# One wait of VectorE a step further back, and four split tiles of eight for three, in the edge stage of a graph network layer

## Chip, cores, metric

The kernel runs on one core of one Trainium2 chip. The metric is the device time of one execution in microseconds (us), here the median of several runs. The engines are TensorE (PE in the profile), VectorE (DVE), ScalarE (ACT), GpSimd (POOL) and SyncE (SP, which issues DMAs). The "PEld" rows of the profile are the weight loads of TensorE.

## What is computed

One layer of a graph network on 1250 nodes with 512 features and 20000 edges with 128 attributes, sorted by their target node:

```python
h = maximum(layernorm(x), 0)                    # node features
msg = relu(h[src] + (edge_attr @ W_edge + b_edge))
aggr = segment_sum(msg, dst, num_segments=N)    # the edge part
g = (1.0 + eps) * h + aggr
g = gelu(layer_norm(g @ W1 + b1, g1, be1))
g = gelu(layer_norm(g @ W2 + b2, g2, be2))
g = layer_norm(h + g, gA, bA)
m = gelu(g @ M1) @ M2
out = x + layer_norm(g + m, gB, bB)
```

Everything is float32. The first three lines are the edge part, with which this text deals; the dense stages follow it.

## The kernel before

**Tiles and groups.** An edge tile is 128 edges. There are 157 of them, in 40 groups of four (the last group has one tile). A group has two pairs of tiles; pair number 2 x group + p, with p 0 or 1, is what one instruction of 128x1024 elements handles. All loops over the groups are written out, so what an engine does stands in a fixed order.

**What happens to a pair.**
- GpSimd gathers the 128 source rows of each tile with an indirect DMA (L630) into `rows`, which has room for three groups. It waits for the z of six pairs back.
- TensorE embeds the pair: `embed` multiplies the attributes by W_edge into one of three PSUM buffers (`ps_u0`, `ps_u1`, `ps_t1`), and waits for the z of three pairs back, which read that buffer.
- VectorE adds the rows to the embedding: `add_rows` writes z (L1161). z has four buffers of a pair each.
- ScalarE makes `msg_hi`, relu(z) rounded to fp32r (L837). VectorE makes `msg_lo`, relu(z) minus msg_hi (L1167).
- TensorE scatters: `visit` (L1422) multiplies `msg_lo` and `msg_hi` by a one-hot matrix that ScalarE builds from the targets (apart L760, onehot L766), and sums into a window of 128 nodes in PSUM. Where a group straddles two windows there is a second one-hot matrix (apart_first L773) and more scatter matmuls, and ScalarE closes one window and opens the next (L784, L797). There are nine such groups: 12, 17, 21, 25, 28, 30, 33, 35 and 37.

**Two ways to embed a tile.** One matmul in fp32 (L1404), which leaves two records of 128x512 in the profile, one for each pass; or three in fp32r (L1386 to L1388), on attributes and weights that were split into a high and a low part. Of the four pairs of two groups (an even one and the odd one behind it), the first tile of the first `SPLIT` pairs goes the second way; all others the first. The split of these tiles is made for two groups at once: ScalarE rounds the attributes to `attr_hi` (L707), VectorE subtracts it from them into `attr_lo` (L1053). Groups 0 and 1 are not split.

**Order on the engines.** VectorE does, in a group: z of pair 0, msg_lo of the pair two before it, in even groups the split of the group two ahead, z of pair 1, msg_lo of the pair two before that. A z waits for the gathered rows, for the embedding, and, since z has four buffers, for a msg_lo (`msg_lo_done`). TensorE does, in a step: the scatter of pair 1 of two groups back, the embedding of pair 1 of the next group and of pair 0 of the one behind it, and the scatter of pair 0 of the group before.

Of the kernel before, what the change touches and what calls it, by code (L numbers as in the profile page):

```python
# [12 lines left out]
ZRING = 4  # L13
ATTRS = 6
ATTR_PAIRS = ATTRS // 2
SPLIT = 3
NG = 4 * -(-EDGES // (4 * EG))
ET = NG * TPG
TP = ET // 2
# [74 lines left out]
def build(nc, A, out):  # L94
# [10 lines left out]
    with ctx:  # L105
        def sb(name, shape, dt=f32, scope=ctx):
            return scope.enter_context(nc.sbuf_tensor(name, shape, dt))

        def sem(name):
            return ctx.enter_context(nc.semaphore(name))  # L110
# [72 lines left out]
        attr_raw = sb("attr_raw", [P, ATTRS, EG], f32, edge)  # L183
        attr_hi = sb("attr_hi", [P, 2, SPLIT * P], f32r, edge)
        attr_lo = sb("attr_lo", [P, 2, SPLIT * P], f32r, edge)
        apart = sb("apart", [P, TPG, P], f32, edge)
# [90 lines left out]
        z_done, msg_hi_done, msg_lo_done = (sem(n) for n in ("z_done", "msg_hi_done", "msg_lo_done"))  # L277
# [82 lines left out]
        def embedded(g, p):  # L360

            return (ps_u[0], ps_u[1], ps_t[1])[g.bank(p)][:, 0:D * g.in_pair(p)]

        def summed(g, p):

            return z[:, (2 * g.k + p) % ZRING, 0:D * g.in_pair(p)]

        def apart_tiles(k):
            return attr_raw[:, k:k + 2, :].rearrange("p g (u e) -> p (g u) e", e=2 * P)[:, 0:SPLIT, 0:P]

# [614 lines left out]
        def _(dve):  # L985
# [167 lines left out]
            def add_rows(g, p):  # L1153
                if g.gr == 0:
                    dve.wait_ge(direct_done, 2 * p + 2)
                else:
                    dve.wait_ge(rows_in[g.slot(p)], 32 * g.lap + 16 * g.in_pair(p))
                dve.wait_ge(emb_done[p], g.gr + 1)
                if 2 * g.gr + p >= 3:
                    dve.wait_ge(msg_lo_done, 2 * g.gr + p - 2)  # L1160
                v.tensor_tensor(summed(g, p), embedded(g, p),  # L1161
                                rows[:, g.r, 2 * p:2 * p + g.in_pair(p), :].rearrange("p a d -> p (a d)"), ALU.add).then_inc(z_done, 1)

# [6 lines left out]
            def group(g):  # L1170
                add_rows(g, 0)
                if not zero(g.gr):
                    msg_low(g.next(-1), 0)
                if g.gr % 2 == 0 and g.gr + 2 < NG:
                    split_attr(g.next(2))
                if g.pairs == 2:
                    add_rows(g, 1)
                if not zero(g.gr):
                    msg_low(g.next(-1), 1)
# [201 lines left out]
        def _(pe):  # L1381
# [8 lines left out]
            def embed(g, p):  # L1390
# [9 lines left out]
                for e in range(g.in_pair(p) - 1, -1, -1):  # L1400
                    place, second = g.half
                    part = 2 * second + p
                    if e or direct or part >= SPLIT:
                        last = t.matmul(o[:, e * D:(e + 1) * D], attr_raw[:, g.k, (2 * p + e) * P:(2 * p + e + 1) * P], we_raw[:, :],  # L1404
# [278 lines left out]
```

## Time and profile before

| | us |
|---|---|
| median of 3 runs | 490.02 (489.7 to 490.27) |
| the profiled execution | 489.55 |
| its span, first to last instruction | 487.5 |
| PE busy | 460.0 |
| DVE busy | 393.1 |
| ACT busy | 310.5 |
| POOL busy | 267.0 |

The edge part lasts up to about 241 us of the span. A row of the profile's timeline gives an instruction's start and how long it took. On VectorE and ScalarE an instruction can start before the one ahead of it has ended, so the distance from start to start tells more than the length. On TensorE a matmul's end is modelled, and again the starts are what counts. "Idle before" is what the profile shows an engine to have waited, with what released it.

### The profile page before, as it was taken

To read this page: it belongs to the slowest core of one execution; us is meant where nothing else is said; L and a number is where in the kernel's file an instruction comes from. 1 tells how busy PE (TensorE), PEld (TensorE's weight loads), DVE (VectorE), ACT (ScalarE), POOL (GpSimd) and SP (SyncE) were. 2 spreads that over 40 slices of the span, in tenths; PEclk is the share of its full clock that TensorE was granted. 3 is DMA by queue.
4 is the path that set the end of the run, shared out by engine and by line. 5 is a ranking of instruction groups with operands and counts; after the bars stand their busy time and mean duration, and the time that the engine had idled before them with its cause. 6 is when DMAs were issued, how large, how long until landed. Compare 5 with 4: busy or idle time off the path is not lost.

```text
span 487.5 us, 7358 instructions
## 1 busy us (share of the span) xinstructions
PE 460.0 (94%) x1927; PEld 340.2 (70%) x1928; DVE 393.1 (81%) x563; ACT 310.5 (64%) x586; POOL 267.0 (55%) x299
## 2 busy tenths in 40 slices
PE   6629999999999999999899999999999999999994
PEld 2205666666666666666678888888888898888883
DVE  6898899999999999899847777789989755752575
ACT  4847788898999999999716555567665672033000
POOL 4867777777777777774015443346553551410342
PEclk9969999999999999999999999999999999999999
DMA  7968899788888878775094232535511240220122
GB/s 266 337 220 271 293 301 316 246 254 248 251 266 268 255 251 247 245 243 158 3 327 149 86 108 87 178 102 172 170 47 65 55 120 0 87 86 0 45 90 82
DMA packets 31430, 85.27 MB, mean 175 GB/s; under 512 B 4609, under 2 KB 4945, under 8 KB 31378
## 3 DMA queue, kind: packets, MB, share of 16 engines
q0 software_dynamic: 12560, 41.17, 27.5%
q1 hardware_dynamic: 18818, 43.51, 26.2%
q8 instruction: 21, 0.34, 0.3%
q14 instruction: 31, 0.25, 0.1%
HBM read 72.08 MB, written 5.24 MB: 159 GB/s over the span
## 4 chain that ended last, share of the span: by engine, by line
PE 37%; DVE 26%; issue 10%; ACT 9%; POOL 6%; DMA 6%; ACTq 2%; DVEq 0%; SPq 0%; POOLq 0%
DVE msg_lo L1167 11%; DVE z L1161 9%; PE ps_u L1386 8%; PE ps_u L1388 8%; PE ps_u L1387 8%; PE ps_t L1386 3%; PE ps_t L1388 3%; PE ps_t L1387 3%; POOL rows L630 3%; ACT msg_hi L837 3%; ACT apart L760 3%; PE ps_t L1539 2%; DMA rows<-gather_table,src_idx 2%; DMA w_raw<-in_W 2%; DMA rows<-in_x,src_idx 1%
## 5 line engine op out<-in xcount | busy, mean ns | idle before, releaser
L630 POOL DMA_INDIRECT rows<-gather_table,src_idx x153 | 152.6, 997 | 46.5 <-issue 46.5
L648 POOL TENSOR_TENSOR var_eps<-mv,eps_t 128x1 f32<-128x1 f32 x40 | 20.6, 515 | 137.8 <-ACT squares L909 80.2
L837 ACT ACTIVATE msg_hi<-z 128x1024 fp32r<-128x1024 f32 (+1 forms) x79 | 82.7, 1047 | 19.9 <-DVE z L1161 19.6
L1167 DVE SCALAR_TENSOR_TENSOR msg_lo<-z,msg_hi 128x1024 fp32r<-128x1024 f32 (+1 forms) x79 | 95.1, 1206 | 0.0
L1161 DVE TENSOR_TENSOR z<-ps_u,rows 128x1024 f32<-128x1024 f32 (+1 forms) x53 | 64.2, 1211 | 9.8 <-PE ps_u L1404 3.1
L1404 PE MATMUL ps_u<-we_raw,attr_raw 128*128 128x512 f32 x134 | 68.0, 617 | 3.5 <-DMA attr_raw<-in_attr_t 3.1
L1386 PE MATMUL ps_u<-w_hi,lhs_lo 128*128 128x512 f32 x160 | 64.5, 403 | 1.6 <-DVE lhs_lo L1230 1.6
L1388 PE MATMUL ps_u<-w_hi,lhs_hi 128*128 128x512 f32 x160 | 62.6, 392 | 0.0
L1387 PE MATMUL ps_u<-w_lo,lhs_hi 128*128 128x512 f32 x160 | 62.3, 390 | 0.0
L1422 PE MATMUL ps_t<-msg_hi,onehot 128*128 128x512 f32 x149 | 58.5, 393 | 0.0
L1422 PE MATMUL ps_t<-msg_lo,onehot 128*128 128x512 f32 x149 | 58.5, 393 | 0.0
L760 ACT ACTIVATE apart<-iota,neg_rel_last 128x128 f32<-128x128 f32 x157 | 49.7, 387 | 0.0
L1404 PEld LDWEIGHTS ps_u<-we_raw,attr_raw 128*128 128x128 f32 x134 | 26.0, 198 | 26.1 <-issue 22.7
L657 POOL TENSOR_TENSOR w_lo<-w_raw,w_hi 128x512 f32 (+1 forms) x24 | 32.3, 1349 | 18.0 <-ACT w_hi L899 13.3
L909 ACT ACTIVATE squares<-work,neg_shift 128x512 f32<-128x512 f32 (+1 forms) x30 | 25.9, 863 | 22.2 <-DVE neg_mean L1255 22.1
L1260 DVE SCALAR_TENSOR_TENSOR work<-ps_u,b 128x1024 f32<-128x1024 f32 (+1 forms) x20 | 19.1, 956 | 22.4 <-PE ps_u L1388 21.8
L1386 PEld LDWEIGHTS ps_u<-w_hi,lhs_lo 128*128 128x128 f32 x160 | 30.1, 188 | 7.7 <-DVE lhs_lo L1230 1.9
L960 ACT ACTIVATE ff_full<-ps_u 128x512 f32<-128x512 f32 (+2 forms) x24 | 12.6, 526 | 35.6 <-PE ps_u L1388 35.6
L1388 PEld LDWEIGHTS ps_u<-w_hi,lhs_hi 128*128 128x128 f32 x160 | 30.0, 188 | 6.6
L1161 DVE TENSOR_TENSOR z<-ps_t,rows 128x1024 f32<-128x1024 f32 x26 | 31.7, 1220 | 3.4 <-PE ps_t L1388 1.0
L1323 DVE TENSOR_TENSOR ff_lo<-ff_full,ff_hi 128x512 fp32r<-128x512 f32 (+2 forms) x24 | 18.2, 779 | 19.9 <-ACT ff_hi L961 19.9
L1387 PEld LDWEIGHTS ps_u<-w_lo,lhs_hi 128*128 128x128 f32 x160 | 30.1, 188 | 5.7
(181 smaller groups left out, 1031.1 us busy)
## 6 DMA issues: line engine op xcount, KB each, us to landing
attr_raw<-in_attr_t SPq DMA_DIRECT2D x20, 512.0 KB, 5.4
w_raw<-in_W SPq DMA_DIRECT2D x24, 256.0 KB, 2.9
tile_in<-mid SPq DMA_DIRECT2D x10, 512.0 KB, 3.6
res<-in_x SPq DMA_DIRECT2D x20, 256.0 KB, 2.7
xin<-in_x SPq DMA_DIRECT2D x5, 512.0 KB, 5.2
out<-work SPq DMA_DIRECT2D x10, 256.0 KB, 2.0
rows<-gather_table,src_idx POOLq DMA_INDIRECT x153, 4.2
gather_table<-tab SPq DMA_DIRECT2D x4, 512.0 KB, 4.4
```

What stands on the lines that cost most here:

```text
L630: g.indirect_dma_start(rows[:, group.r, e % TPG, :], None, gather_table[:, :], bass.IndirectOffsetOnAxis(src_idx[:, e:e + 1].bitcast(u32), ...
L657: g.tensor_tensor(w_lo[1 - s % 2][:, cols], w_raw[:, p, :], w_hi[1 - s % 2][:, cols].bitcast(f32), ALU.subtract).then_inc(w_lo_done, 1)
L760: last = a.activation(apart[:, e, :], iota[:, 0:P], ACT.Square, bias=neg_rel_last[:, ds(g.gr, 1), e:e + 1].rearrange("p a e -> p (a e)"))
L837: a.activation(pair(msg_hi, g, p), summed(g, p), ACT.Relu).then_inc(msg_hi_done, 1)
L909: a.activation(squares[:, first:first + width], x, ACT.Square, bias=neg_shift[:, slot:slot + 1], scale=float(width) ** -0.5, accum_out=mv[ ...
L1161: v.tensor_tensor(summed(g, p), embedded(g, p), rows[:, g.r, 2 * p:2 * p + g.in_pair(p), :].rearrange("p a d -> p (a d)"), ALU.add).then_i ...
L1167: v.scalar_tensor_tensor(pair(msg_lo, g, p), summed(g, p), 0.0, pair(msg_hi, g, p).bitcast(f32), ALU.max, ALU.subtract).then_inc(msg_lo_do ...
L1386: t.matmul(o, lhs[1][cols], rhs[0][rcols], start=first, stop=False)
L1387: t.matmul(o, lhs[0][cols], rhs[1][rcols], start=False, stop=False)
L1388: return t.matmul(o, lhs[0][cols], rhs[0][rcols], start=False, stop=last)
L1404: last = t.matmul(o[:, e * D:(e + 1) * D], attr_raw[:, g.k, (2 * p + e) * P:(2 * p + e + 1) * P], we_raw[:, :], start=alone_in_bank, stop= ...
L1422: last = t.matmul(summed_in(bank), selection[:, e, :], m[:, g.r, e * D:(e + 1) * D], start=False, stop=(e == end and m is msg_hi), skip_gr ...
```

## The change

```diff
@@ -13,7 +13,7 @@
-SPLIT = 3
+SPLIT = 4
@@ -1156,8 +1156,8 @@
                 dve.wait_ge(emb_done[p], g.gr + 1)
-                if 2 * g.gr + p >= 3:
-                    dve.wait_ge(msg_lo_done, 2 * g.gr + p - 2)
+                if 2 * g.gr + p >= 4:
+                    dve.wait_ge(msg_lo_done, 2 * g.gr + p - 3)
                 v.tensor_tensor(summed(g, p), embedded(g, p),
```

The z of pair n waited for the msg_lo of pair n - 3, which is what VectorE did just before it; now it waits for that of pair n - 4, the last reader of the buffer of z that it writes. And `SPLIT` is 4: the first tile of pair 1 of odd groups is embedded in three fp32r matmuls too, and `attr_hi` and `attr_lo` are made of 128x512 elements, not 128x384.

The order of TensorE's instructions, at the step in which pair 7 (group 3, in ps_u) and pair 8 (group 4, in ps_t) are embedded:

```order
 L1422 MATMUL ps_t<-msg_lo,onehot 128x512
 L1422 MATMUL ps_t<-msg_hi,onehot 128x512
-L1404 MATMUL ps_u<-we_raw,attr_raw 128x512 x2
+L1404 MATMUL ps_u<-we_raw,attr_raw 128x512
+L1386 MATMUL ps_u<-we_hi,attr_lo 128x512
+L1387 MATMUL ps_u<-we_lo,attr_hi 128x512
+L1388 MATMUL ps_u<-we_hi,attr_hi 128x512
 L1404 MATMUL ps_t<-we_raw,attr_raw 128x512
 L1386 MATMUL ps_t<-we_hi,attr_lo 128x512
```

One fp32 matmul of pair 7 has become three of fp32r; the same occurs at every odd group from 3 to 37.

VectorE's order from the msg_lo of pair 0 on, before, with the semaphores that each instruction waits for:

```order
L1167 SCALAR_TENSOR_TENSOR msg_lo<-z,msg_hi 128x1024 [waits msg_hi_done]
L1161 TENSOR_TENSOR z<-ps_u,rows 128x1024 [waits msg_lo_done,emb_done1,rows_in3]
L1167 SCALAR_TENSOR_TENSOR msg_lo<-z,msg_hi 128x1024 [waits msg_hi_done]
L1161 TENSOR_TENSOR z<-ps_u,rows 128x1024 [waits msg_lo_done,emb_done0,rows_in4]
L1167 SCALAR_TENSOR_TENSOR msg_lo<-z,msg_hi 128x1024 [waits msg_hi_done]
L1053 TENSOR_TENSOR attr_lo<-attr_raw,attr_hi 128x384 [waits emb_done0,attr_hi_done]
L1161 TENSOR_TENSOR z<-ps_t,rows 128x1024 [waits msg_lo_done,emb_done1,rows_in5]
```

The same place after the change:

```order
L1167 SCALAR_TENSOR_TENSOR msg_lo<-z,msg_hi 128x1024 [waits msg_hi_done]
L1161 TENSOR_TENSOR z<-ps_u,rows 128x1024 [waits emb_done1,rows_in3]
L1167 SCALAR_TENSOR_TENSOR msg_lo<-z,msg_hi 128x1024 [waits msg_hi_done]
L1161 TENSOR_TENSOR z<-ps_u,rows 128x1024 [waits msg_lo_done,emb_done0,rows_in4]
L1167 SCALAR_TENSOR_TENSOR msg_lo<-z,msg_hi 128x1024 [waits msg_hi_done]
L1053 TENSOR_TENSOR attr_lo<-attr_raw,attr_hi 128x512 [waits emb_done0,attr_hi_done]
L1161 TENSOR_TENSOR z<-ps_t,rows 128x1024 [waits msg_lo_done,emb_done1,rows_in5]
```

No instruction has moved. The z of pair 3 waits for no msg_lo any more, every later one for a count that is one lower, and attr_lo is wider.

## Rows read from the trace of the kernel before

**Rows 1.** The page, busy us, share of the span and count of each engine.
```profile
PE 460.0 (94%) x1927; PEld 340.2 (70%) x1928; DVE 393.1 (81%) x563; ACT 310.5 (64%) x586; POOL 267.0 (55%) x299
```
**Rows 2.** Windows: length, busy us of each engine, granted clock, DMA share, GB/s.
```profile
100.00:150.00 50.00, 49.91 (x177) 32.77 (x177) 48.00 (x45) 45.12 (x89) 38.12 (x40) 1.00 0.83 259
```
**Rows 3.** The chain that ended last, 48 to 176 us: start, us, what.
```profile
48.51 8.52 DMA rows<-gather_table,src_idx
57.05 1.22 DVE z L1161
...
129.09 1.21 DVE z L1161
...
139.34 1.21 DVE z L1161
...
175.03 1.24 DVE z L1161
```
**Rows 4.** Timeline of DVE, 127 to 133 us: start, us, engine, line, operation, tiles.
```profile
127.45 1.21 DVE L1167 SCALAR_TENSOR_TENSOR msg_lo<-z,msg_hi 128x1024 fp32r<-128x1024 f32 x1
128.58 0.58 DVE L1053 TENSOR_TENSOR attr_lo<-attr_raw,attr_hi 128x384 fp32r<-128x384 f32 x1
129.09 1.21 DVE L1161 TENSOR_TENSOR z<-ps_u,rows 128x1024 f32<-128x1024 f32 x1
130.22 1.21 DVE L1167 SCALAR_TENSOR_TENSOR msg_lo<-z,msg_hi 128x1024 fp32r<-128x1024 f32 x1
131.56 1.23 DVE L1161 TENSOR_TENSOR z<-ps_t,rows 128x1024 f32<-128x1024 f32 x1
```
**Rows 5.** Timeline of PE, embeds in 119 to 132 us (x2: one fp32 matmul).
```profile
119.60 1.88 PE L1404 MATMUL ps_t<-we_raw,attr_raw 128*128 128x512 f32 x4
...
121.32 1.02 PE L1404 MATMUL ps_u<-we_raw,attr_raw 128*128 128x512 f32 x2
...
124.70 1.02 PE L1404 MATMUL ps_u<-we_raw,attr_raw 128*128 128x512 f32 x2
...
126.25 1.02 PE L1404 MATMUL ps_t<-we_raw,attr_raw 128*128 128x512 f32 x2
...
129.65 2.74 PE L1404 MATMUL ps_u<-we_raw,attr_raw 128*128 128x512 f32 x6
```
**Rows 6.** Timeline of PE, the same embed three periods apart, and the end.
```profile
62.36 0.79 PE L1386 MATMUL ps_u<-we_hi,attr_lo 128*128 128x512 f32 x1
...
93.10 0.79 PE L1386 MATMUL ps_u<-we_hi,attr_lo 128*128 128x512 f32 x1
...
240.22 0.49 PE L1422 MATMUL ps_t<-msg_lo,onehot 128*128 128x512 f32 x1
240.55 0.39 PE L1422 MATMUL ps_t<-msg_hi,onehot 128*128 128x512 f32 x1
```
**Rows 7.** Timeline of DVE, the last two z; in brackets the idle time before.
```profile
233.43 1.22 DVE L1161 TENSOR_TENSOR z<-ps_t,rows 128x1024 f32<-128x1024 f32 x1 [1.00 <-PE ps_t L1388]
...
235.92 0.69 DVE L1161 TENSOR_TENSOR z<-ps_u,rows 128x512 f32<-128x512 f32 x1
```
**Rows 8.** Timeline of ACT behind 176 us, and its wait for z in 104:176.
```profile
176.29 1.06 ACT L837 ACTIVATE msg_hi<-z 128x1024 fp32r<-128x1024 f32 x1 [0.26 <-DVE z L1161]
...
188.36 0.62 ACT L766 ACTIVATE onehot<-apart 128x512 fp32r<-128x512 f32 x1
188.88 0.51 ACT L707 ACTIVATE attr_hi<-attr_raw 128x384 fp32r<-128x384 f32 x1
...
237.94 0.62 ACT L837 ACTIVATE msg_hi<-z 128x512 fp32r<-128x512 f32 x1
...
ACT msg_hi L837 <- DVE z L1161: 5.8, 12, 0.7
```
**Rows 9.** Timeline of POOL's gathers, z of pair 57, and rows in 100:230.
```profile
161.82 1.17 POOL L630 DMA_INDIRECT rows<-gather_table,src_idx  x1 [0.30 <-issue]
...
172.06 1.16 POOL L630 DMA_INDIRECT rows<-gather_table,src_idx  x1 [0.30 <-issue]
...
180.31 1.21 DVE L1161 TENSOR_TENSOR z<-ps_u,rows 128x1024 f32<-128x1024 f32 x1
...
DMA to landing us min/median/max: 3.5/4.1/5.8
```

## What the change should do

> **What bounds the kernel now.** I read the page's busy shares first. TensorE is busy for 94% of the span [rows 1], but the edge part of the kernel, up to about 241 us, has three more engines near the top: in 100 to 150 us PE is busy 49.91 us of 50, DVE 48.00, ACT 45.12 [rows 2]. So a share settles nothing, and I went to the chain of waits. From 57 to 176 us it is VectorE alone, z and msg_lo in turn [rows 3]. The first z there, at 57.05, is pair 9; it had waited for gathered rows issued at 48.51. From there one period of two groups (four pairs) takes 139.34 - 129.09 = 10.25 us [rows 3].
>
> The DVE timeline shows what the 10.25 consists of [rows 4]. msg_lo to attr_lo, start to start, is 128.58 - 127.45 = 1.13; attr_lo to z is 0.51; z to msg_lo is 1.13; and msg_lo to z is 131.56 - 130.22 = 1.34. The same msg_lo lets the next instruction start after 1.13 where that is attr_lo and after 1.34 where it is z. The z behind a msg_lo waits for just that msg_lo; the z behind attr_lo waits for it too, but it has long finished. So 0.21 us of each such z is VectorE waiting for its own previous write, three times in a period.
>
> TensorE is almost level with it. Its period in quiet groups is 129.65 - 119.60 = 10.05 us, with no idle time reported [rows 5]. Before the first window switch (group 12) it is held to VectorE's pace: three periods from 62.36 to 93.10 take 30.74 instead of 3 x 10.05 = 30.15 [rows 6]. Behind that every switch of node window adds four or eight scatter matmuls, TensorE falls behind and streams; from 104 us on I find no hole in its starts until the last scatter at 240.55 [rows 6]. It is TensorE that VectorE waits for at the end: the z at 233.43 sat idle for 1.00 us [rows 7]. So VectorE bounds the first third of the edge part, TensorE's total the rest, and both have to shrink for the end to move.
>
> **The change, part by part.** (1) The split of the fourth embed. Per pair of groups one fp32 matmul becomes three fp32r ones. A pair embedded with two fp32 matmuls takes 121.32 - 119.60 = 1.72 us of TensorE, one with one fp32 and three fp32r takes 126.25 - 124.70 = 1.55 [rows 5]: 0.17 less. It concerns pair 1 of each odd group from 3 to 37, 18 pairs. Two of them, pairs 7 and 11, are embedded before the z at 57.05, which waits for rows whatever TensorE does; 16 count: 16 x 0.165 = 2.6 us (1.72 - 1.555, both ends read to 0.01). TensorE's quiet period becomes 9.89.
>
> (2) The relaxed wait. The z now waits for the msg_lo two back, which ended one z earlier. It saves 0.21 x 3 = 0.63 per period where VectorE is the bound. No row shows a z directly behind a msg_lo without the wait; the bounds are 1.34 (nothing gained) and 1.13, the step behind every other instruction of this size. I take 1.13, since the z behind attr_lo has all its other waits too and starts 0.51 behind an instruction of 0.58.
>
> (3) The wider split on VectorE: 128x512 instead of 128x384, 19 times, 16 of them behind 57 us. The nearest rows are z with 512 columns, 0.69, against z with 1024, 1.22: about 1.0 ns a column, so +0.13 each [rows 7]. Bounds: +0.10 (ACT's slope, next) to +0.18. VectorE's period is then 10.25 - 0.63 + 0.13 = 9.75, just below TensorE's 9.89, so it stops being the bound and TensorE gets back what VectorE held up: 30.74 - 30.15 = 0.59 us. That is the second term.
>
> (4) The wider split on ScalarE: attr_hi with 384 columns takes 0.51, onehot with 512 takes 0.62 [rows 8]: +0.10 each. ScalarE waits for z at 176.29 for the last time [rows 8] and then runs without a wait for another engine's data through the msg_hi of the last pair at 237.94. Five splits lie in that stretch: +0.5 us on it. It pays only if ScalarE can't begin that stretch sooner. In 104 to 176 us it waited 5.8 us for z, so it can take z's that come earlier, less 0.7 us for its seven splits there. I cost it at nothing; if the cover is gone it is 0.5.
>
> (5) The gathered rows. GpSimd's issues run free: eight rows, two groups, in 172.06 - 161.82 = 10.24 us [rows 9], and nothing in the change moves them. VectorE can't keep a pace of 9.75 for good. The second row of pair 57 is issued at 172.06 and its z starts at 180.31, so the row has 8.2 us, and lands in 4.1 (median) to 5.8 us (longest) [rows 9]. So z's can come some 4.1 us earlier, 2.4 by the longest. The shift that TensorE allows is 3.2 at the end and 2.3 or less up to pair 53, so this hides, with less than 1 us to spare in the last pairs.
>
> Sum: 2.6 + 0.6 = 3.2 us off the end of the edge part. At that end TensorE's last matmul starts 240.22 and 240.55, and ScalarE and VectorE lag by under 1 us; behind it stand the dense stages, which TensorE fills and which start from this end, so the shift is kept. The profiled execution took 489.55 us (span 487.5 plus 2.05 around it); it becomes 486.35. The median of the runs is 490.02, 0.47 more, so the forecast for the median is 490.02 - 3.2 = **486.8 us**.
>
> **A rule against it.** The rows show 0.21 us for the wait [rows 4]. The Trainium skill, "VectorE: DVE Perf Modes", section "The DRAIN you can't avoid", says that a chain of eight copies with a semaphore behind each took as long as one with none but the last, that "the semaphore costs nothing extra here". By it the z would start 1.34 behind msg_lo with or without the wait, and the change would bring what the third rival below has. The trace doesn't agree: 1.13 against 1.34 behind the same msg_lo.
>
> **Rivals.** A. The forecast: 486.8, from 486.2 to 487.4 by the bounds of the terms.
>
> B. The gain is clipped, since a third engine becomes the bound. ScalarE's stretch from 176.29: it gets its z's 3 us earlier but pays 0.5 and perhaps some of the 0.7, so 2.0 to 2.7 are left: 487.3 to 488.0. Or a few late rows: with landings of 5.8 in the last pairs the shift is 2.4 there, 487.6. For it: ScalarE is busy 45 of 50 us already [rows 2]. Against it: 5.8 us of waits that can be used up. I put it at 487.8.
>
> C. The wait was not the cause of the 0.21, so VectorE keeps 1.34 and pays 0.13 per period: 10.38. The z of pair 55 at 175.03 [rows 3] has 11 splits between it and 57 us and comes 11 x 0.13 = 1.4 us later; ScalarE's stretch starts that much later and is 0.5 longer, 1.9; with some 0.7 us of slack at the end 1.2 are left: 491.2, slower. TensorE's shorter total brings nothing then, because its last scatters wait for msg_hi and msg_lo. It decides from a step msg_lo to z of about 1.30 on: then the period isn't shorter than 10.25. Against it stand the rows of 4.
>
> D. Only the wait pays: the fp32r triple costs what the fp32 matmul did (say behind a later weight load). Then TensorE's total stays and the 0.6 us is left: 489.4, no change. Against it: the 0.17 repeats at each pair of rows 5.
>
> E. More than forecast: TensorE also waits a little for VectorE between the switches, in holes too small for me to see, and the shift reaches the 4.1 us that the rows allow: 485.9.
>
> **How the numbers follow.** A 0.55, B 0.17, C 0.05, D 0.09, E 0.14. The likeliest is A: 486.8. The range leaves out C, most of D and the far edge of E: 485.7 to 488.8. A measurement of this kernel tells 0.2%, 1.0 us, from no change: faster is below 489.0, slower above 491.0. Faster: A, B, E and a part of C and D that comes out mixed, 0.86; same, most of D and half of C: 0.10; slower: 0.04.
>
> **What would show it.** In the profile after: step (2), the DVE timeline in 120 to 180 us has z 1.13 behind msg_lo, and its idle time moves to waits for rows or for PE. Step (1): PE's quiet period of two groups is 9.89, all embeds take 1.55. Step (3): attr_lo with 512 columns lasts about 0.71, and the three periods behind 62 us take 29.7 instead of 30.74. Step (4): ScalarE's last wait for z comes before 173 us. Step (5): waits of z for rows appear, but the last scatter starts at about 237.3 instead of 240.55. The prediction is wrong if z stays at 1.34, if TensorE shows holes in 180 to 237 us (a third engine rules), or if the stages behind don't keep the shift.

## The result, and the profile after

The changed kernel takes 520.2 us (median of 4 runs), the kernel before 490.1 beside it: ratio 1.0615, interval 1.0585 to 1.0645. It is 30 us slower, where 3 us less was forecast. The profiled execution took 523.66 us with a span of 521.5. Here and below a ratio is taken from the undisturbed (fast) executions of both kernels, the medians from all of them, so the two can differ a little.

The page of the changed kernel: busy shares [rows 1], TensorE's granted clock in 40 slices, the chain by engine, and three groups of instructions (count, busy us, mean ns, idle us before them and its releaser).

```profile
PE 470.7 (90%) x1945; PEld 345.0 (66%) x1946; DVE 392.2 (75%) x563; ACT 313.3 (60%) x586; POOL 306.6 (59%) x299
...
PEclk9969979999989999989999999999999999999998
...
PE 37%; POOL 28%; DMA 11%; issue 10%; DVE 9%; ACT 2%; ACTq 1%; SPq 0%; POOLq 0%; DVEq 0%
...
L630 POOL DMA_INDIRECT rows<-gather_table,src_idx x153 | 191.5, 1252 | 46.5 <-issue 43.7
...
L1161 DVE TENSOR_TENSOR z<-ps_u,rows 128x1024 f32<-128x1024 f32 (+1 forms) x53 | 64.2, 1211 | 25.4 <-DMA rows<-gather_table,src_idx 23.8
...
L1161 DVE TENSOR_TENSOR z<-ps_t,rows 128x1024 f32<-128x1024 f32 x26 | 31.8, 1221 | 21.6 <-DMA rows<-gather_table,src_idx 21.6
```

Only one engine is busier by much: GpSimd, 306.6 us in place of 267.0. Nearly all of it (38.9 us) is in one group, the 153 row gathers, whose issue takes 1252 ns in the mean (997 before). POOL now holds 28% of the chain, and VectorE's z's wait 45.4 us for rows. TensorE has less to do than before and still shows 10.7 us more. Part of it is the granted clock. The 7 and the two 8s behind it in the PEclk row are three stretches at half the clock (1.2 GHz): 66.0 to 72.9, 144.6 to 148.0 and 229.9 to 233.3 us. Each began during or 0.4 us behind a wait of TensorE for z, of 3.05, 3.36 and 1.88 us. The kernel before has none of them in its edge part; the 6 of the third slice stands in its page too. That is a consequence of the late z's, not their cause.

The same stretch as [rows 2] (length, then busy us of PE, PEld, DVE, ACT, POOL, granted clock, DMA share, GB/s):

```profile
100.00:150.00 50.00, 39.64 (x131) 24.86 (x132) 37.62 (x36) 35.97 (x72) 40.55 (x32) 0.97 0.66 198
```

PE, DVE and ACT lost 9 to 10 us each of 50; only POOL gained, and it issued 32 instructions in place of 40.

Now VectorE's timeline, to be read against [rows 4], and GpSimd's in the same microseconds (start, us; in brackets the idle time before):

```profile
129.70 1.22 DVE L1161 TENSOR_TENSOR z<-ps_u,rows 128x1024 f32<-128x1024 f32 x1 [1.94 <-DMA rows<-gather_table,src_idx]
130.84 1.22 DVE L1167 SCALAR_TENSOR_TENSOR msg_lo<-z,msg_hi 128x1024 fp32r<-128x1024 f32 x1
131.97 1.22 DVE L1161 TENSOR_TENSOR z<-ps_t,rows 128x1024 f32<-128x1024 f32 x1
133.10 1.22 DVE L1167 SCALAR_TENSOR_TENSOR msg_lo<-z,msg_hi 128x1024 fp32r<-128x1024 f32 x1
```
```profile
130.25 0.94 POOL L630 DMA_INDIRECT rows<-gather_table,src_idx  x1 [0.30 <-issue]
131.50 1.38 POOL L630 DMA_INDIRECT rows<-gather_table,src_idx  x1 [0.31 <-issue]
133.18 1.96 POOL L630 DMA_INDIRECT rows<-gather_table,src_idx  x1 [0.30 <-issue]
```

The z starts 131.97 - 130.84 = 1.13 us behind msg_lo, as forecast. But look at the issues. The one at 131.50 started while the msg_lo of 130.84 ran; it ended at 132.88, which is 0.82 us after that msg_lo's end (130.84 + 1.22 = 132.06). The next started at 133.18, 0.08 us into the next msg_lo, and ended at 135.14: again 0.82 after the end of it (134.32).

**The rule that the rows give (theory P below).** An issue takes 0.95 us and the next starts 0.30 later. If it starts more than 0.05 us into a running msg_lo or attr_lo, the VectorE instructions here that have two inputs in SBUF, it ends 0.82 us after that instruction, so it takes up to 1.99. Beside z, with one input in PSUM, it takes 0.95. The rule was worked out from these two traces. From 55 us to the last z it gives the length within 0.1 us for all 132 issues of the kernel before and for 133 of 136 after; the other three start 0.04 to 0.05 us into a msg_lo and were held as well. Above 1.0 us (called held below) are 19 issues before, with 5.9 us in sum over 0.95, and 65 after, with 41.8 us.

Why did the kernel before suffer so little? Its rows in 118 to 124 us, GpSimd and then VectorE:

```profile
118.34 0.95 POOL L630 DMA_INDIRECT rows<-gather_table,src_idx  x1 [0.30 <-issue]
119.60 0.95 POOL L630 DMA_INDIRECT rows<-gather_table,src_idx  x1 [0.30 <-issue]
120.85 1.17 POOL L630 DMA_INDIRECT rows<-gather_table,src_idx  x1 [0.30 <-issue]
122.32 0.95 POOL L630 DMA_INDIRECT rows<-gather_table,src_idx  x1 [0.30 <-issue]
123.57 0.94 POOL L630 DMA_INDIRECT rows<-gather_table,src_idx  x1 [0.30 <-issue]
```
```profile
119.99 1.21 DVE L1167 SCALAR_TENSOR_TENSOR msg_lo<-z,msg_hi 128x1024 fp32r<-128x1024 f32 x1
121.33 1.23 DVE L1161 TENSOR_TENSOR z<-ps_u,rows 128x1024 f32<-128x1024 f32 x1
122.47 1.22 DVE L1167 SCALAR_TENSOR_TENSOR msg_lo<-z,msg_hi 128x1024 fp32r<-128x1024 f32 x1
123.82 1.22 DVE L1161 TENSOR_TENSOR z<-ps_t,rows 128x1024 f32<-128x1024 f32 x1
```

Two free issues take 2 x 1.25 = 2.50 us, and VectorE's pair step with the wait is 122.47 - 119.99 = 2.48. The two run in step: one issue starts just before a msg_lo (122.32 against 122.47), which does not hold it, the next falls on its end. One issue in eight (120.85) falls inside and is held; that puts GpSimd back in step, and 7 x 1.25 + 1.47 = 10.22 is, to 0.02, the period that I had read in [rows 9] as GpSimd's own pace. Without the 0.21 us of wait the step is 2.27. A held issue ends 0.82 after its msg_lo and the next starts 0.30 later, so 1.22 + 0.82 + 0.30 = 2.34 us behind that msg_lo's start. The next msg_lo starts 2.27 behind it: 0.07 us sooner, and it holds that issue as well. With the wait it started 2.48 behind, 0.14 us too late to hold it. Without it GpSimd issues one row per step where two are used up, until VectorE has to wait for rows.

TensorE's embeds on the other hand came out as meant. Two neighbouring pairs with one fp32 matmul each start 1.57 apart, where such a pair and one with two fp32 matmuls took 1.55 and 1.72 [rows 5]; the last scatter of the edge part starts at 275.25, against 240.55 [rows 6].

```profile
122.34 1.02 PE L1404 MATMUL ps_u<-we_raw,attr_raw 128*128 128x512 f32 x2
...
123.91 1.02 PE L1404 MATMUL ps_t<-we_raw,attr_raw 128*128 128x512 f32 x2
...
275.25 0.40 PE L1422 MATMUL ps_t<-msg_hi,onehot 128*128 128x512 f32 x1
```

### The profile page after: what moved, and what is told of

Same layout as the page of the kernel before. It is cut to its first block, busy times and chain, and to the rows that moved or that the text cites. A ratio compares the mean times of both kernels' runs of the same rounds, so it can differ in the third digit from the quotient of the medians.

```text
span 521.5 us, 7394 instructions
## 1 busy us (share of the span) xinstructions
PE 470.7 (90%) x1945; PEld 345.0 (66%) x1946; DVE 392.2 (75%) x563; ACT 313.3 (60%) x586; POOL 306.6 (59%) x299
## 4 chain that ended last, share of the span: by engine, by line
PE 37%; POOL 28%; DMA 11%; issue 10%; DVE 9%; ACT 2%; ACTq 1%; SPq 0%; POOLq 0%; DVEq 0%
POOL rows L630 26%; PE ps_u L1386 8%; PE ps_u L1388 8%; PE ps_u L1387 8%; DMA rows<-gather_table,src_idx 7%; PE ps_t L1386 4%; PE ps_t L1388 4%; PE ps_t L1387 3%; PE ps_t L1539 2%; DVE z L1161 2%; DMA w_raw<-in_W 2%; DMA rows<-in_x,src_idx 1%; DMA xin<-in_x 1%; DVE work L1245 1%; POOL w_lo L657 1%
## 5 line engine op out<-in xcount | busy, mean ns | idle before, releaser
L630 POOL DMA_INDIRECT rows<-gather_table,src_idx x153 | 191.5, 1252 | 46.5 <-issue 43.7
L837 ACT ACTIVATE msg_hi<-z 128x1024 fp32r<-128x1024 f32 (+1 forms) x79 | 82.8, 1048 | 50.7 <-DVE z L1161 50.2
L1404 PE MATMUL ps_u<-we_raw,attr_raw 128*128 128x512 f32 x110 | 59.7, 634 | 10.7 <-DVE z L1161 6.6
L1422 PE MATMUL ps_t<-msg_lo,onehot 128*128 128x512 f32 x149 | 59.9, 402 | 0.7 <-DVE msg_lo L1167 0.5
L1404 PE MATMUL ps_t<-we_raw,attr_raw 128*128 128x512 f32 x54 | 30.1, 643 | 13.5 <-DVE z L1161 13.5
L1386 PE MATMUL ps_u<-we_hi,attr_lo 128*128 128x512 f32 x50 | 40.0, 801 | 0.3 <-DVE z L1161 0.3
L1404 PEld LDWEIGHTS ps_u<-we_raw,attr_raw 128*128 128x128 f32 x110 | 20.6, 198 | 26.1 <-issue 14.1
L1422 PEld LDWEIGHTS ps_t<-msg_lo,onehot 128*128 128x128 f32 x149 | 28.7, 192 | 9.6 <-issue 3.2
```

The costliest lines, as they stand in the source:

```text
L630: g.indirect_dma_start(rows[:, group.r, e % TPG, :], None, gather_table[:, :], bass.IndirectOffsetOnAxis(src_idx[:, e:e + 1].bitcast(u32), ...
L837: a.activation(pair(msg_hi, g, p), summed(g, p), ACT.Relu).then_inc(msg_hi_done, 1)
L1386: t.matmul(o, lhs[1][cols], rhs[0][rcols], start=first, stop=False)
L1422: last = t.matmul(summed_in(bank), selection[:, e, :], m[:, g.r, e * D:(e + 1) * D], start=False, stop=(e == end and m is msg_hi), skip_gr ...
```

## The experiments

One plain fact has to stand first, or the numbers can't be read. The kernel before took 489 to 492 us in some jobs and 531 to 543 in others, on every run of a job. I call these the lower and the upper level. Each result is given with the kernel before of its own job, and times of different levels are not compared. What is known of the levels stands at the end of this section.

**1. One part alone (upper level).** The wait relaxed, three tiles split:

```diff
-                if 2 * g.gr + p >= 3:
-                    dve.wait_ge(msg_lo_done, 2 * g.gr + p - 2)
+                if 2 * g.gr + p >= 4:
+                    dve.wait_ge(msg_lo_done, 2 * g.gr + p - 3)
```

> Only the relaxed wait; the fourth tile is not split. Theory P (port): a gather issue of GpSimd that starts while a VectorE instruction with two SBUF inputs (msg_lo, attr_lo) is already running for more than 0.05 us ends only 0.82 us after that instruction, where it takes 0.95 us otherwise. With the wait a pair on VectorE steps by 2.49 us, almost the 2.51 of two issues, and the issues stay where they collide little (19 of 131 long, 5.9 us over in 57 to 227 us); without it the natural step is 2.28 and the issues slide over msg_lo (65 of 136 long, 42 us over). So this kernel has most of the loss: 505 to 520 us, mean issue above 1.15 us. Theory S (split): the loss comes from the fourth split (wider attr_lo, more fp32r matmuls): 488 to 490 us, mean issue about 1.0 us.

And the fourth tile split, the wait as before:

```diff
-SPLIT = 3
+SPLIT = 4
```

> Only the fourth split; z waits for the msg_lo right ahead as before. Theory P: VectorE's step per pair stays at 2.49 and the issues keep their places: 490 to 492 us, mean issue about 1.0 us; the pace of two groups is 10.38 and not 10.25. Theory S: 515 us or more.

Measured: 519.2 us with the relaxed wait, 534.9 with the fourth split, the kernel before 535.9; ratios 0.966 (0.958 to 0.975) and 0.996 (0.992 to 1.001). So the relaxed wait alone was 3% faster there. Neither theory had that. In absolute time it stands where the changed kernel does, and its trace has as many held issues: 61 of 135, 38.5 us in sum. A second time, beside a kernel before of 539.3:

> The relaxed wait alone once more, for a chip on which the kernel before takes 490. Theory P: 510 to 520 us, 60 or so long issues. Theory S (the fourth split makes the loss): 488 to 490.

Measured: 524.4 us, 0.971 (0.961 to 0.981), 62 of 135 issues held, 37.9 us. At the lower level the relaxed wait was never measured by itself.

**2. The hold taken away.** The changed kernel, but msg_lo is max(z, 0) with a running sum into an unused column. It leaves out the subtraction of msg_hi, so it has one SBUF input and the same 1.2 us:

```diff
-                v.scalar_tensor_tensor(pair(msg_lo, g, p), summed(g, p), 0.0, pair(msg_hi, g, p).bitcast(f32),
-                                       ALU.max, ALU.subtract).then_inc(msg_lo_done, 1)
+                v.tensor_scalar(pair(msg_lo, g, p), summed(g, p), 0.0, 0.0, ALU.max, ALU.add,
+                                accum_out=sums[:, 2 * g.gr + p:2 * g.gr + p + 1]).then_inc(msg_lo_done, 1)
```

> The changed kernel, but msg_lo reads z alone (relu of z with a running sum, not minus msg_hi), so that it has one SBUF input; its output is not the reference's in that part. Same waits, same number of instructions and almost the same length. Theory P: only attr_lo can still hold an issue, fewer than 20 long ones, mean issue at most 1.02 us, and the time is what the prediction had: 485.5 to 488.5 us. Rival D (DMA): the issues are long since the rings or the memory are busy whatever VectorE reads: 515 us or more.

> The changed kernel with a msg_lo that reads z alone (relu of z with a running sum, without msg_hi, so its output differs in that part), once more. Theory P: no issue is held by msg_lo, all take 0.95 us, and where the kernel before takes 490 this one takes 485.5 to 488.5. Rival D (the DMAs are slow, not the issue): 515 or more even with short issues.

Measured, upper level: 536.0 beside 535.9 us (0.999, 0.996 to 1.003) and 539.2 beside 539.3 (1.000, 0.996 to 1.004). The time did not follow, yet the trace of the first shows the mechanism: 66 issues started more than 0.05 us inside a msg_lo, 57 of them early enough to be held by the rule, and not one was longer than 0.95.

**3. A msg_lo that waits for the z ahead (upper level).** The changed kernel, with a gap put in front of msg_lo:

```diff
+                if 2 * g.gr + p + 3 < 2 * NG:
+                    dve.wait_ge(z_done, 2 * g.gr + p + 3)
                 v.scalar_tensor_tensor(pair(msg_lo, g, p), summed(g, p), 0.0, pair(msg_hi, g, p).bitcast(f32),
```

> The changed kernel, but msg_lo also waits for the z right ahead of it, so that the gap of 0.21 us stands ahead of msg_lo and not ahead of z. Theory P: what counts is VectorE's step per pair, 2.49 again: 490 to 493 us, few long issues. Rival G: the gap between msg_lo and z itself is what lets GpSimd in; that is still closed: 510 us or more.

Measured: 538.0 us, 1.005 (1.001 to 1.009); 29 of 133 issues held. The holds fell, though not to the few that P had; the time is that of the upper level and tells nothing.

**4. Both kernels again, in one job (lower level).** No edit.

> The kernel before, unchanged, for its trace on the chip of these runs: it took 490 us where the change was measured and 535.9 where the first four experiments ran. Theory P (gather issues held by msg_lo) has 490 us and a mean issue of 1.00 us, wherever the kernel runs. Rival M (something of the machine adds to every kernel whose VectorE is not held back by the gathers): 530 us or more with a mean issue near 1.05 us, and waits whose data had long been ready.

> The changed kernel, unchanged, beside the one before on the same chip. Theory P: 519 to 522 us with 60 or more long issues, on either chip, so that it is slower than before by 6% where before takes 490 and faster by 3% where before takes 535.

Measured: 491.3 beside 490.5 us (1.001, 0.998 to 1.003) and 519.6 (1.058, 1.054 to 1.062). The result stands; 62 of 136 issues were held, 38 us.

**5. The wait relaxed for one pair in four (upper level).** In the one kernel for n % 4 == 0, in the other for n % 4 == 3, three tiles split:

```diff
+                n = 2 * g.gr + p
+                if n >= 3:
+                    dve.wait_ge(msg_lo_done, n - 3 if n % 4 == 0 else n - 2)
```

> The kernel before with the wait relaxed for one z in four, that of pair 0 of even groups; split of three tiles. Theory P worked through with the rule (an issue that starts more than 0.05 us into a two-input instruction ends 0.82 us after it): this one lets the issues find places that collide little, 489 to 493 us. Rival Q (each relaxed wait costs its share, wherever it is): a third of the loss of the relaxed wait, about 500 us, and the same as the next kernel.

> The same for another z in four, that of pair 1 of odd groups. Theory P, by the same rule: the issues have no such places, 505 to 520 us. Rival Q: about 500 us, like the kernel before this one.

Measured: 530.0 and 529.6 us beside 539.3 (0.981, 0.973 to 0.990; 0.982, 0.975 to 0.988). They did not differ; the rule fits every issue (42 and 37 held), but P's expectation of two different times was not borne out. At the lower level neither was measured.

**6. The hold taken away and the fourth split, again.** Two jobs, both at the upper level, so they told nothing new:

> The changed kernel with msg_lo computed from one SBUF input (max(z, 0) and a running sum, without subtracting msg_hi), a third time: it leaves the subtraction out, so its messages are not the reference's. Theory P (a row gather that GpSimd issues while a msg_lo or attr_lo with two SBUF inputs runs ends only 0.82 us after it): nearly all issues take 0.95 us here, so where the kernel before takes 490 us this one takes 484 to 489 us, as the changed kernel was forecast. Rival R (the gathers' lead itself, not the long issues, is what costs): 515 us or more even where the kernel before takes 490. Where the kernel before takes 535 to 539 us, both expect 534 to 540 us, as measured twice, and nothing is told apart.

> The fourth split tile alone, the wait as before. Where the kernel before takes 490 us: theory P, with VectorE still waiting 1.34 us behind each msg_lo, keeps its pair step near 2.5 us and GpSimd's issues in step with it: 488 to 492 us. Rival S (the wider attr_lo alone puts the issues out of step): 505 to 520 us. Where the kernel before takes 535 to 539 us: 533 to 538 us, as measured once.

> The changed kernel with msg_lo computed from one SBUF input (it leaves the subtraction of msg_hi out). It has not yet run on a chip where the kernel before takes 490 us. There, theory P (an issue of GpSimd that falls into a msg_lo with two SBUF inputs ends only 0.82 us behind it, and this alone turned the forecast gain into a loss) expects 484 to 489 us, all issues at 0.95 us; rival R (the shorter step itself, or the gathers' lead, costs) expects 505 us or more with the same 0.95 us issues. Where the kernel before takes 535 us or more, both expect 533 to 540 us and some 4,000 semaphore records in the trace in place of 6,050.

> The fourth split tile alone, wait as before, on a chip where the kernel before takes 490 us: theory P expects the pair step to stay at 2.5 us, since the 0.21 us waits stay, and 487 to 492 us; rival S (the wider attr_lo alone puts the issues out of step with VectorE) 505 to 520 us, with over 50 issues above 1.0 us. Where the kernel before takes 535 us or more: 532 to 538 us.

Measured: one input 537.1 beside 536.2 (1.002, 0.998 to 1.006) and 535.9 beside 537.5 (1.002, 0.998 to 1.006); fourth split 534.3 (0.996, 0.992 to 1.001) and 535.0 (0.999, 0.996 to 1.003).

**7. The hold taken away, lower level.** The kernel of 2 once more:

> The changed kernel with msg_lo computed from one SBUF input (it leaves the subtraction of msg_hi out), by itself beside the kernel before, with no third program. On a chip or beside programs where the kernel before takes 490 us, theory P expects 484 to 489 us and rival R 505 us or more. If the kernel before takes 535 us or more again: 533 to 540 us, and then the number of programs beside it is not what sets its level.

Measured: 488.4 us beside 491.1, ratio 0.994 (0.992 to 0.996). This is the deciding run: both parts of the change are in, VectorE's step is 2.27, and the loss of 30 us is a gain of 2.7 (by the interval 1.8 to 3.7). GpSimd's group on its page, and its issues beside a msg_lo:

```profile
L631 POOL DMA_INDIRECT rows<-gather_table,src_idx x153 | 147.3, 963 | 46.5 <-issue 42.8
```
```profile
119.83 0.95 POOL L631 DMA_INDIRECT rows<-gather_table,src_idx  x1 [0.30 <-DVE z L1162]
...
122.34 0.95 POOL L631 DMA_INDIRECT rows<-gather_table,src_idx  x1 [0.30 <-issue]
```
```profile
119.53 1.20 DVE L1168 TENSOR_SCALAR_CACHE_REDUCE msg_lo<-z 128x1024 fp32r<-128x1024 f32 x1
...
121.80 1.20 DVE L1168 TENSOR_SCALAR_CACHE_REDUCE msg_lo<-z 128x1024 fp32r<-128x1024 f32 x1
```
```profile
237.88 0.40 PE L1423 MATMUL ps_t<-msg_hi,onehot 128*128 128x512 f32 x1
```

The issues at 119.83 and 122.34 start 0.30 and 0.54 us into a msg_lo and take 0.95. 62 issues started more than 0.05 us inside a msg_lo, 53 of them early enough to be held by the rule; none was. Of 8 that fell into an attr_lo, which still has two SBUF inputs, 7 were held; the eighth started late enough to take 0.95 by the rule too. The last scatter starts at 237.88.

**8. The whole computation, one SBUF input (lower level).** z stays in its PSUM bank; msg_lo reads it there and msg_hi from SBUF. The wait before z goes, and TensorE's embed has to wait for the msg_lo that reads its bank:

```diff
-            return z[:, (2 * g.k + p) % ZRING, 0:D * g.in_pair(p)]
+            return embedded(g, p)
...
-                if 2 * g.gr + p >= 4:
-                    dve.wait_ge(msg_lo_done, 2 * g.gr + p - 3)
...
-                    pe.wait_ge(z_done, 2 * g.gr + p - 2)
+                    pe.wait_ge(msg_lo_done, 2 * g.gr + p - 2)
```

> The changed kernel with z kept in the PSUM bank that the embedding was summed in, so that msg_lo reads one input from PSUM and one from SBUF; the wait on a msg_lo before z goes, and TensorE's embed waits for the msg_lo three pairs back where it waited for the z. Everything is computed. Theory P (only two SBUF inputs hold an issue) expects almost all issues at 0.95 us beside msg_lo and, where the kernel before takes 490 us, 484 to 492 us (the chain from a msg_lo over embed, z and two further steps is some 6.4 us for three pairs, under TensorE's 7.3, but embed can now come late). Rival R (the length of the step or msg_lo itself, whatever its inputs) expects held issues of up to 1.97 us again and 510 us or more.

Measured: 676.0 us beside 489.8, ratio 1.379 (1.375 to 1.384). As a kernel it failed, for a reason of its own. VectorE, and TensorE behind it:

```profile
118.90 1.22 DVE L1165 SCALAR_TENSOR_TENSOR msg_lo<-ps_u,msg_hi 128x1024 fp32r<-128x1024 f32 x1
122.10 1.23 DVE L1159 TENSOR_TENSOR ps_u<-ps_u,rows 128x1024 f32<-128x1024 f32 x1 [1.99 <-PE ps_u L1386]
```
```profile
124.60 1.23 PE L1402 MATMUL ps_t<-we_raw,attr_raw 128*128 128x512 f32 x2 [2.61 <-DVE msg_lo L1165]
```
```profile
119.26 0.94 POOL L630 DMA_INDIRECT rows<-gather_table,src_idx  x1 [3.24 <-DVE ps_u L1159]
```

The msg_lo at 118.90 has the full operation of the kernel, with one input from PSUM. The issue at 119.26 starts 0.36 us into it and takes 0.94. Of 67 issues that started inside a msg_lo, each early enough to be held by the rule, not one was. All 16 that started inside an attr_lo were above 1.0, by little (1.08 at most). So it is the second SBUF input that holds, not the operation, its length or its output. The 676 us come from the new wait: VectorE works msg_lo two pairs behind z, so the msg_lo three pairs back stands behind the z of the pair before, and the embed can't start until that z is through. TensorE and VectorE take turns, with idle times of 2.61 and 1.99 us; the expectation of 484 to 492 us had missed that, and was wrong.

**9. The fourth split alone, lower level.**

> The fourth split tile alone, wait as before, by itself beside the kernel before. Theory P expects the pair step to stay at 2.5 us, since the 0.21 us waits stay, and 487 to 492 us; rival S (the wider attr_lo alone puts the issues out of step with VectorE) 505 to 520 us, with over 50 issues above 1.0 us. If the kernel before takes 535 us or more here, nothing is told apart, and the number of programs in a job doesn't set its level.

Measured: 493.0 us beside 489.9, ratio 1.004 (1.002 to 1.007): 3.1 us slower by the medians, 1 us beyond what P allowed. VectorE over one period, and the held issue in it:

```profile
120.39 1.21 DVE L1161 TENSOR_TENSOR z<-ps_u,rows 128x1024 f32<-128x1024 f32 x1
121.53 1.21 DVE L1167 SCALAR_TENSOR_TENSOR msg_lo<-z,msg_hi 128x1024 fp32r<-128x1024 f32 x1
...
130.12 0.74 DVE L1053 TENSOR_TENSOR attr_lo<-attr_raw,attr_hi 128x512 fp32r<-128x512 f32 x1
130.78 1.21 DVE L1161 TENSOR_TENSOR z<-ps_u,rows 128x1024 f32<-128x1024 f32 x1
```
```profile
122.25 1.30 POOL L630 DMA_INDIRECT rows<-gather_table,src_idx  x1 [0.30 <-issue]
```
```profile
242.69 0.39 PE L1422 MATMUL ps_t<-msg_hi,onehot 128*128 128x512 f32 x1
```

The period is 130.78 - 120.39 = 10.39 us, 0.14 longer than the 10.25 of [rows 3], and the wider attr_lo is that: 0.64 to 0.66 to the z behind it in place of 0.51. GpSimd stays in step: one issue in eight is held, now for 1.30 in place of 1.17, 18 of 133 in all. VectorE bounds the whole edge part: from 92 us on no z waits for more than 0.15 us, where in the kernel before some behind 195 us waited for TensorE (1.00 us at the longest [rows 7]). So TensorE's shorter embeds give nothing and the longer period costs 16 x 0.13 = 2.1 us, less those waits: from the z of pair 9 to the last scatter it is 242.69 - 57.75 = 184.94 us in place of 240.55 - 57.05 = 183.50. That is 1.4 of the 3.1 us; another 0.7 stands ahead of that z. This is the mechanism of the prediction's rival C, made by keeping the wait.

**10. The change kept, the step lengthened.** 0.22 us of useless work in the place of the wait:

```diff
                     dve.wait_ge(msg_lo_done, 2 * g.gr + p - 3)
+                    if (2 * g.gr + p) % 4 != 1:
+                        v.tensor_tensor(pad[:, (2 * g.gr + p) % 4, :], embedded(g, p)[:, 0:PAD], rows[:, g.r, 2 * p, 0:PAD], ALU.add)
```

> The changed kernel, both parts in, with useless work in the place of the wait: before each z but the one behind attr_lo, VectorE adds 152 columns of the same embedding and rows into an unused buffer (one PSUM and one SBUF input, some 0.22 us), so that its pair step is 2.49 us again in place of 2.27. Theory P (the step's length against the 2.50 us of two issues decides which issues fall into a msg_lo) expects the issues in step again, under 25 of 132 above 1.0 us, and 491 to 496 us, some 25 us faster than the changed kernel for more work on VectorE. Rival R (the wait's absence or the wider tiles themselves cost, or VectorE's load) expects 515 us or more.

Measured: 535.8 us beside 535.8 (0.999, 0.996 to 1.003). It fell at the upper level, so its time decides nothing. Its trace does say something of the step. VectorE and GpSimd:

```profile
128.36 1.21 DVE L1165 TENSOR_TENSOR z<-ps_u,rows 128x1024 f32<-128x1024 f32 x1
129.50 1.21 DVE L1171 SCALAR_TENSOR_TENSOR msg_lo<-z,msg_hi 128x1024 fp32r<-128x1024 f32 x1
130.63 0.30 DVE L1164 TENSOR_TENSOR pad<-ps_u,rows 128x152 f32<-128x152 f32 x1
130.85 1.21 DVE L1165 TENSOR_TENSOR z<-ps_u,rows 128x1024 f32<-128x1024 f32 x1
```
```profile
127.72 1.31 POOL L632 DMA_INDIRECT rows<-gather_table,src_idx  x1 [0.30 <-issue]
129.34 0.95 POOL L632 DMA_INDIRECT rows<-gather_table,src_idx  x1 [0.30 <-issue]
130.59 0.94 POOL L632 DMA_INDIRECT rows<-gather_table,src_idx  x1 [0.30 <-issue]
```

The step is 130.85 - 128.36 = 2.49 again, and the issue at 129.34 starts 0.16 before its msg_lo and is free. Of 134 issues 28 were held (17.1 us), as with the fourth split alone at this level (27 to 29, 14 to 15 us), where the relaxed wait without the filling had 61 and 62. So with the step back at its old length half of the holds are gone, though the wait is as relaxed as before. That this brings the changed kernel back to some 493 us was not shown.

**The two levels, and what stays open.** Kernel before (of each job's runs, lowest to highest), and which experiments ran beside it:

| kernel before | beside it |
|---|---|
| 489.7 to 491.5 | the changed kernel |
| 489.5 to 492.0 | e5, e6 |
| 489.8 to 491.9 | e16 |
| 489.0 to 491.4 | e18 |
| 489.4 to 492.4 | e19 |
| 531.4 to 540.1 | e1, e2, e3, e4 |
| 535.6 to 543.1 | e7, e9, e10, e11 |
| 531.9 to 539.7 | e12, e13 |
| 530.7 to 541.1 | e14, e15 |
| 534.3 to 539.6 | e20 |

In ten of the twelve traces of the upper level (e9's left out) VectorE stands still 6 to 10 times in the edge part for 2.6 to 6.8 us, without waiting for rows, often some 19 to 25 us apart. Apart from (8), with its own cause, no trace of the lower level has one. One of these stalls, in the kernel of e12; VectorE, ScalarE, and SyncE's queue:

```profile
84.85 1.23 DVE L1162 TENSOR_TENSOR z<-ps_u,rows 128x1024 f32<-128x1024 f32 x1 [4.22 <-issue]
```
```profile
84.86 1.06 ACT L838 ACTIVATE msg_hi<-z 128x1024 fp32r<-128x1024 f32 x1 [5.06 <-remote]
```
```profile
84.79 0.33 SPq L454 DMA_DIRECT2D attr_raw<-in_attr_t  x1
```

Three engines go on at the same moment, though the embed that this z reads had ended at 77.9, and the profile finds no releaser: "issue" or "remote" stands where a semaphore should. By the code all three wait there for the semaphore of a group's second embed. In these traces many of the semaphore events are missing: 3,817 to 4,720 are recorded where those of the lower level have 6,049 to 6,055 (the profiled execution of e9 was disturbed and is left out). The kernels whose gathers run far ahead have most of these stalls (in the kernel of e3 some 16 us from the issue of a pair's second row to its z). Where the gathers are late there are few: one and two in the two traces of the relaxed wait (4 to 5 us from issue to z), and it takes 519 and 524 us there, as the changed kernel does at the lower level. So the relaxed wait seems to have won at the upper level because the kernel before lost more; the kernel before itself has no trace at that level. Neither the chip nor the number of programs in a job sets the level: e16 and e14 ran on one chip, e18 and e20 on another, and e20 had as few programs beside it as e16. What does, and whether the stall comes from late semaphore events, stays open. An engineer who had met the upper level only would have called the relaxed wait a gain of 3%.

## Why the prediction was wrong, by its steps

Step (5) failed: "GpSimd's issues run free: eight rows, two groups, in 172.06 - 161.82 = 10.24 us [rows 9], and nothing in the change moves them." They did not run free. The rows quoted for it carried the sign: 1.17 and 1.16 us [rows 9] where the issues between them take 0.95. A pace that equals VectorE's period to 0.01 us is not an engine's own pace; GpSimd's own is 8 x 1.25 = 10.0. The change moved every msg_lo against these issues. It shortened VectorE's pair step to 2.27, below the 2.50 that two rows need even when free, and put each msg_lo just in front of the issue that follows a held one. Taking the hold away turned 30 us of loss into 2.7 of gain (7), at the level of the result; what is left of rival explanations, the shorter step or the lead of the gathers by itself, falls with that run. It leaves a subtraction out; (8), which computes everything, shows the missing hold but not the time.

The other steps, one by one:

- The sum: right, once the hold is gone. The median of (7) is 2.7 us lower, its last scatter 240.55 - 237.88 = 2.67 sooner. Its profiled execution had 3.4 us at the lower clock right behind the edge part, which the one before had not; e5, the kernel before once more, had them too, and against it the last scatter is 240.99 - 237.88 = 3.11 sooner and the span 3.3 us shorter. The forecast was 3.2. But this is partly luck, since both of its terms were off, in opposite directions:

```profile
58.42 1.10 PE L1404 MATMUL ps_u<-we_raw,attr_raw 128*128 128x512 f32 x2 [0.44 <-DVE z L1161]
...
233.17 0.40 PE L1386 MATMUL ps_u<-we_hi,attr_lo 128*128 128x512 f32 x1
```
```profile
59.11 1.02 PE L1405 MATMUL ps_u<-we_raw,attr_raw 128*128 128x512 f32 x2
...
117.99 1.02 PE L1405 MATMUL ps_t<-we_raw,attr_raw 128*128 128x512 f32 x2
...
230.09 0.40 PE L1387 MATMUL ps_u<-we_hi,attr_lo 128*128 128x512 f32 x1
```
```profile
240.99 0.40 PE L1422 MATMUL ps_t<-msg_hi,onehot 128*128 128x512 f32 x1
```

- (1) TensorE's shorter embed: right in kind, somewhat too large. The rows are of the kernel before, of (7) and of e5. From the embed at 119.60 [rows 5] (117.99 in (7)) to the last one (233.17 and 230.09) the lead grows from 1.61 to 3.08 us, with 11 shortened pairs: 0.13 each, 2.1 us for 16 in place of 2.6. The quiet period is 9.92 (117.99 to 127.91) where 9.89 was forecast.
- (2) The relaxed wait: the cause and the size of the 0.21 were right, z stands 1.13 behind msg_lo. What TensorE got back was put too low. At 58.42 the embed of (7) is 0.69 us behind (59.11), at 119.60 it is 1.61 ahead; 5 shortened pairs give 0.7 of these 2.3 us, and 1.6 is left for this term (1.5 if e5 is compared), where 0.6 was forecast from the three periods behind 62 us alone.
- (3) The wider attr_lo: right, +0.13 a period, shown by itself in (9).
- (4) The wider attr_hi: hidden, as forecast, once the hold is gone. In (7) it takes 0.61 to 0.62 us in place of 0.51, ScalarE waits for a z the last time at 171.2 us (forecast: before 173), and the edge part still ends sooner. In the changed kernel ScalarE waited for z all along (50.2 us), which tells nothing.
- The lead of 8.2 us that a row had over its z was taken as a store to draw on. It is one only while GpSimd can refill it.
- No rival was the right one. B had late rows, but as a clipping of about 1 us; C had a loss, by a wait that did go away.

The Trainium skill, "VectorE: DVE Perf Modes", section "The DRAIN you can't avoid", would have kept z at 1.34. The trace after has 1.13, so it does not hold for this wait.

The page of the Trainium skill that bears on the true cause is "SBUF — State Buffer", section "Who interferes with whom". It says that a VectorE instruction with two SBUF inputs contends with a GpSimd instruction that reads SBUF, and one with at most one does not, outside the 2-port perf modes. The traces agree: held beside msg_lo from two SBUF buffers, not held in 62 and 67 cases (7, 8) beside the same step with one. The same section infers that making descriptors needs the shared write interface and so isn't disturbed by tensor_tensor. Here the measurement decides otherwise: issues beside attr_lo, a tensor_tensor, were held in 7 of 8 cases in (7) and in 16 of 16 in (8).

## What to carry to other kernels

When a cheap instruction on a side engine shows two durations (0.95 and 1.17 us here), find out what the longer one overlaps before you call the engine free. And when two engines have the same period to 0.01 us, one is holding the other: work out what each does alone, and what the phase between them becomes once one is made faster. A wait that looks like waste on the bounding engine may be what keeps another engine's issues out of its way; a step shorter than what the gathers need (two issues of 1.25 us) can be kept up only as long as their lead lasts.

## What the runs showed of the hardware

- The hold lasts beyond the VectorE instruction: the issue ends 0.82 us behind it. The rule gives an issue's length within 0.1 us in all but 7 of the 2,540 issues from 55 us to the last z in 19 traces (e9's left out). Some 0.04 us of start decide between 0.95 and up to 2.00 us: issues that started up to 0.03 us into such an instruction were free but for two beside an attr_lo in e20, and those that started 0.05 to 0.09 us into one were all held.
- An issue that starts before the VectorE instruction is not held (122.32 against 122.47 before).
- The effect feeds itself where the step is 2.27: held issues follow one another until VectorE runs out of rows (65 of 136 held, 45.4 us of waits for rows).
- Unchanged kernels can have two levels, 490 and 535 us, constant within a job, and the traces of the upper one have 3,817 to 4,720 semaphore records in place of some 6,050.
